# Triangle attention in front of a Mamba-like layer: turned weights in two PSUM banks of their own, projections between a row's other products

## What is computed

```python
q = (xn @ w_q).reshape(B, I, J, H, C) * (1.0 / np.sqrt(C))
k = (xn @ w_k).reshape(B, I, J, H, C)
v = (xn @ w_v).reshape(B, I, J, H, C)
scores = jnp.einsum('bimhc,binhc->bihmn', q, k) + tri_bias + mask_bias
attn = jax.nn.softmax(scores, axis=-1)
o = jnp.einsum('bihmn,binhc->bimhc', attn, v)
g = jax.nn.sigmoid((xn @ w_g + b_g).reshape(B, I, J, H, C))
o = (g * o).reshape(B, I, J, H * C)
return o @ w_o + b_o
...
x = x + _L0_conv_ref(_gn(x), ...)
x = x + _L1_conv_ref(_gn(x), ...)
```

## Time and profile before

| | |
|---|---|
| median of 3 runs | 27614.51 us (27614.04 to 27621.61) |
| profiled execution | 27622.95 us, its span 27621.2 us |
| mean granted TensorE clock | 0.946 |
| busy over the span | PE 79%, DVE 92%, ACT 86%, GpSimd (POOL) 85% |
| attention stage | from about 700 to 2910 us of the span |
| the second layer with the normalisation ahead of it | from 2910 us to the end |

### The profile page before, as it was taken

The page is one execution under the profiler, slowest core; times in us unless marked ns, Lnnn a source line. Parts: engine busy times, 40 slices in busy tenths (PEclk is TensorE's granted clock), DMA queues, the critical chain, the costliest instruction groups (busy, mean ns, idle before and its releaser), DMA issues.

```text
span 27621.2 us, 494663 instructions
## 1 busy us (share of the span) xinstructions
PE 21957.3 (79%) x145198; PEld 16882.3 (61%) x145198; DVE 25285.8 (92%) x23743; ACT 23632.0 (86%) x48522; POOL 23358.9 (85%) x10372
## 2 busy tenths in 40 slices
PE   5888588788887888887888888888788888888887
PEld 1666366666666666666666666666666666666666
DVE  7777599999999999999999999999999999999998
ACT  2677488988989988889898898888898998888988
POOL 4000399999999999999999999999999999999999
PEclk6999799999999999999999999999999999999999
DMA  4111433333333333333333333333333333333333
GB/s 148 48 46 46 150 105 106 107 105 107 106 107 107 107 106 107 106 107 105 107 106 106 106 108 105 108 104 108 105 107 105 108 104 108 106 106 107 106 107 97
DMA packets 2189148, 2868.62 MB, mean 104 GB/s; under 512 B 695002, under 2 KB 964858, under 8 KB 2177786
## 3 DMA queue, kind: packets, MB, share of 16 engines
q1 hardware_dynamic: 2181978, 2803.33, 33.0%
q10 hardware_dynamic: 4608, 33.82, 0.3%
HBM read 2667.01 MB, written 169.74 MB: 103 GB/s over the span
## 4 chain that ended last, share of the span: by engine, by line
ACT 28%; PE 25%; issue 18%; DVE 12%; POOL 4%; ACTq 1%; DVEq 1%; DMA 0%; SPq 0%; POOLq 0%
DVE hst L1530 11%; PE yps L1240 7%; ACT dbT L1420 6%; ACT dA L1398 6%; ACT dAs L1398 6%; PE dbx L1225 5%; PE misc L1140 5%; POOL hc L1607 2%; POOL dbu L1593 2%; DVE hc L1538 2%; ACT vab L1353 1%; PE misc L1159 1%; PE misc L1176 1%; PE cps L1216 1%; ACT vab L1339 1%
## 5 line engine op out<-in xcount | busy, mean ns | idle before, releaser
L1593 POOL TENSOR_TENSOR dbu<-dtu,bb 128x1024 f32<-128x1024 f32 x4096 | 9697.6, 2374 | 1209.2 <-DVE hst L1530 1208.3
L1530 DVE TENSOR_TENSOR_SCAN hst<-dA,dbu 128x1024 f32<-128x1024 f32 x4096 | 9336.8, 2279 | 778.1 <-ACT dA L1398 755.9
L1607 POOL TENSOR_TENSOR hc<-hst,cc 128x1024 f32<-128x1024 f32 x4096 | 9743.1, 2379 | 5.6 <-DVE hst L1530 3.7
L1240 PE MATMUL yps<-ident,hc 128*128 128x128 f32 x65536 | 8944.2, 283 | 328.6 <-POOL hc L1607 325.1
L1240 PEld LDWEIGHTS yps<-ident,hc 128*128 128x128 f32 x65536 | 7982.1, 147 | 1824.7 <-issue 1273.4
L1530 DVE TENSOR_TENSOR_SCAN hst<-dAs,dbx 128x1024 f32<-128x1024 f32 x3584 | 8104.2, 2261 | 63.5 <-issue 61.2
L1225 PE MATMUL dbx<-ident,dbT 128*128 128x128 f32 x28672 | 4153.0, 292 | 3329.9 <-DVE hst L1530 2975.1
L1225 PEld LDWEIGHTS dbx<-ident,dbT 128*128 128x128 f32 x28672 | 3391.2, 148 | 4750.2 <-DVE hst L1530 3639.0
L1420 ACT ACTIVATE dbT<-dtuT,bT 128x256 f32<-128x256 f32 x14336 | 6125.1, 495 | 18.2
L1398 ACT ACTIVATE dA<-dtv,aneg 128x508 f32<-128x508 f32 x8192 | 5291.6, 678 | 400.0 <-DVE hst L1530 396.1
L1398 ACT ACTIVATE dAs<-dtv,aneg 128x508 f32<-128x508 f32 x7168 | 4743.7, 710 | 531.0 <-DVE hst L1530 528.8
(11 more groups left out here) (187 smaller groups left out, 25145.4 us busy)
## 6 DMA issues: line engine op xcount, KB each, us to landing
bb<-l_bscr SPq DMA_DIRECT2D x1024, 1024.0 KB, 5.7
cc<-l_bscr SPq DMA_DIRECT2D x1024, 1024.0 KB, 5.5
bx<-l_bscr SPq DMA_DIRECT2D x1024, 256.0 KB, 6.1
xg<-xgp SPq DMA_DIRECT2D x512, 85.0 KB, 2.5
xgp<-xb ACTq DMA_DIRECT2D x32, 1032.0 KB, 9.4
xt<-in_x_dram SPq DMA_DIRECT2D x128, 256.0 KB, 2.7
l_xnT<-xo SPq DMA_DIRECT2D x128, 256.0 KB, 2.0
xn<-l_xnT SPq DMA_DIRECT2D x256, 128.0 KB, 2.1
```

The source lines that it names most:

```text
L1240: mm = pe.matmul(yps[:, p, f * P:(f + 1) * P], hc[:, u % HB, f * 512 + p * P:f * 512 + (p + 1) * P], ident[:], is_transpose=True, start=fi ...
L1530: nc.vector.tensor_tensor_scan(hst[:, v % 4, way], decays.rearrange("p f c -> p (f c)")[:, way], inputs.rearrange("p f c -> p (f c)")[:, way],
L1593: nc.gpsimd.tensor_tensor(to, dtu[:, step % 2], row.unsqueeze(1).to_broadcast([P, 2, 512]), ALU.mult).then_inc(s_inp, 1)
L1607: nc.gpsimd.tensor_tensor(hc[:, v % HB].rearrange("p (f c) -> p f c", f=2), hst[:, v % 4].rearrange("p (f c) -> p f c", f=2), row.unsqueez ...
```

## The change

It has five parts, all in the attention stage.

1. The turned weights go to banks 6 and 7: heads 0 and 2 to bank 6, heads 1 and 3 to bank 7. Scores keep banks 2 to 5 for themselves and wait for the additions of the row before (`s_sm`), no longer for weight copies. Heads 2 and 3 are turned once heads 0 and 1 are copied. The turned factors share bank 6, the sums share bank 0 with q and k, and the output shares bank 1 with v and gate.
2. VectorE copies heads 0 and 2, ScalarE heads 1 and 3, each between additions or exponentials of the next row.
3. q and k of the next row are projected between heads 1 and 2 of the turned weights, v and gate of the next row at the turn's end; a new stage "next" of a turn does so. SyncE loads `xn` two rows ahead and the mask one row ahead, in two functions.
4. PE's turn begins with the scores. ScalarE's tanh comes first in its turn, the factors' copy ahead of the last exponentials.
5. The residual is added by transposes (`is_transpose=True`) in place of matmuls with the identity.

```diff
-            ps_qk, ps_vg, ps_o, ps_x = (banks[:, b] for b in (0, 1, 6, 7))
+            ps_qk, ps_vg = banks[:, 0], banks[:, 1]
+            ps_out, ps_o = banks[:, 1, 0:N], banks[:, 0, 0:N]
+            ps_f = banks[:, 6, 0:N]
...
+                    def project_qk(r, h):
                         pe.wait_ge(s_xn[h], turns(r, h, 1))
-                        wait(pe, s_qe, r)
+                        wait(pe, s_gs, r - 2)
                         for k in range(2):
                             mm = pe.matmul(ps_qk[:, k * N:(k + 1) * N], wqk[:, k], xn[:, h], start=True, stop=True)
                         mm.then_inc(s_qk, 1)
+                    def project_vg(r, h):
                         wait(pe, s_ve, r * 2)
+                        wait(pe, s_xe, r - 2)
...
                     def scores(r, h):
                         pe.wait_ge(s_mk[h], NH * turns(r, h, 1))
                         pe.wait_ge(s_qe, r + 1)
-                        wait(pe, s_tv, r * 3)
-                        wait(pe, s_ta, r)
+                        wait(pe, s_sm, r * NH)
...
+                    def turned(r, h, d):
+                        pe.wait_ge(s_ex, r * NH + (d + 1))
+                        if d == 0:
+                            wait(pe, s_fc, r)
+                        elif d == 2:
+                            pe.wait_ge(s_tv, r * 2 + 1)
+                        else:
+                            wait(pe, s_ta, r * 2 + d // 2)
+                        for k in range(NT):
+                            for a in range(NT):
+                                mm = pe.transpose(banks[:, 6 + d % 2, (k * NT + a) * P:(k * NT + a + 1) * P],
+                                                  ss[:, h, d, a, k * P:(k + 1) * P], ident0[:])
+                        mm.then_inc(s_tf, 1)
...
-                            pe.matmul(dst, wo0[:], goT[:, h, a * P:(a + 1) * P], start=True, stop=False)
-                            mm = pe.matmul(dst, xr[:, h, a], ident0[:], start=False, stop=True)
+                            pe.matmul(dst, wo0[:], goT[:, h, a * P:(a + 1) * P], start=True, stop=False, skip_group_check=True)
+                            mm = pe.matmul(dst, xr[:, h, a], ident0[:], is_transpose=True, start=False, stop=True, skip_group_check=True)
...
+                        if "new" in stages:
+                            scores(r, h)
+                        if "mid" in stages:
+                            turned(r - 1, 1 - h, 0)
+                            turned(r - 1, 1 - h, 1)
+                        if "next" in stages:
+                            project_qk(r + 1, 1 - h)
+                        if "mid" in stages:
+                            turned(r - 1, 1 - h, 2)
+                            turned(r - 1, 1 - h, 3)
+                        if "end" in stages:
+                            output(r - 2, h)
+                        if "next" in stages:
+                            pe.wait_ge(s_qe, r + 2)
+                        if "mid" in stages:
+                            sums(r - 1, 1 - h)
+                            turn_factors(r - 1)
+                        if "next" in stages:
+                            project_vg(r + 1, 1 - h)
```

More of the change, by code:

```diff
@@ L357, in all_rows @@
             def all_rows(eng, turn):
-                turn(0, 0, ("new",))
-                turn(1, 1, ("new", "mid"))
+                every = ("next", "new", "mid", "end")
+                turn(0, 0, ("next", "new"))
+                turn(1, 1, ("next", "new", "mid"))
                 for r in (2, 3, 4):
[L362 to L365, removed]
+                    turn(r, r % 2, every)
+                with eng.Fori(2, N // 2 - 2) as i:
+                    turn(2 * i + 1, 1, every)
+                    turn(2 * i + 2, 0, every)
+                turn(N - 3, 1, every)
+                turn(N - 2, 0, every)
                 turn(N - 1, 1, ("new", "mid", "end"))
@@ L420, in project @@
                         mm.then_inc(s_vg, 1)
[L422 to L442, removed]
                     def scores(r, h):
@@ L511, in turn, with copy_qk @@
                             wait(act, s_bn, r - 3)
-                            nc.scalar.activation(xo1[:, h], ps_x[:, N:2 * N], ACT.Identity, bias=bo[:]).then_inc(s_xe, 1)
+                            nc.scalar.activation(xo1[:, h], ps_out, ACT.Identity, bias=bo[:]).then_inc(s_xe, 1)
                         if "new" in stages:
[L514 to L526, removed]
+                            weights(2)
+                        if "mid" in stages:
+                            act.wait_ge(s_gt, r)
+                            wait(act, s_gs, r - 1)
+                            nc.scalar.mul(fT[:], ps_f, 0.5).then_inc(s_fc, 1)
+                        if "new" in stages:
+                            weights(3)
+                    def copy_qk(r, h):
+                        act.wait_ge(s_qk, r + 1)
+                        nc.scalar.mul(qk[:, h, 0], ps_qk[:, 0:N], float(-1.0 / HD ** 0.5))
+                        nc.scalar.copy(qk[:, h, 1], ps_qk[:, N:2 * N]).then_inc(s_qe, 1)
+                    copy_qk(0, 0)
                     all_rows(act, turn)
@@ L565, in turn @@
                             nc.vector.tensor_tensor(ge[:, h], vg[:, :, 1], bg[:].unsqueeze(1).to_broadcast([P, NT, P]), ALU.add).then_inc(s_ve, 1)
+                            top(0)
                         if "mid" in stages:
+                            turn_out(0)
                             factors(r - 1, 1 - h)
                         if "new" in stages:
[L569 to L575 removed]
+                            top(1)
+                        if "mid" in stages:
+                            turn_out(2)
+                        if "new" in stages:
+                            top(2)
+                            top(3)
                         if "mid" in stages:
```

91 lines of the change are left out of this document (56 added, 35 removed).

## The result

The changed kernel takes 27468.84 us (median of 5 runs, 27458.93 to 27479.74) against 27616.67 of the kernel before on the same chips: a ratio of 0.9945, interval 0.9931 to 0.9960. That is 148 us less, where the forecast of 27285 took 332 off, and lies above the range that ended at 27400.

A forecast was written before the change was run, and what follows sets the result against it. It took the attention stage's ring of waits over four shared banks, once a turn of 8.60 us, as the bound. Turns of 7.3 gave (8.60 - 7.30) x 256 = 333 us off, so 27285, range 27215 to 27400.

The forecast's parts named there:

- everything behind it is untouched: Code after the attention stage, about 700 to 2910 us, was taken as unchanged, with no time of its own.
- Prologue and tail do the same turns as before: Turns outside the attention loop were taken as unchanged, with no time added.
- The ring: Attention stage: waits from scores through ACT's copies to v and gate, closing last at 7.24 us.
- a restart: PE's sums in the attention turn: 0.10 us added to their 1.00 after the wait.
- which I price the same: PE's scores: 1.30 us kept, with a tile-form change on either side instead of one and a restart.
- 0.2 in two turns for the jump: Where the attention loop comes round: 0.2 us for the jump and its registers, giving 7.34 a turn.
- Dearer handoffs: Rival: waits between engines in the attention stage cost more, 7.75 us a turn, 27397 us; chance 0.16.
- the 6.95 of that rival: Rival: PE bounds the attention turn, 6.83 us of work plus one tile change, 27192 us; chance 0.06.
- The clock rival: Rival: the kernel gets slower through the clock; chance 0.03.
- that of no gain: Rival: fT late on ACT delays gating and bank release, turn back at 8.6 us, 27614; chance 0.03.
- Part (4) at nothing: Residual by transposes on PE: worth 0.22 us a turn, costed at nothing because PE would wait before the sums.
- Part (3) and SP: Heads 2 and 3 wait for copies; SP's mask lands 4.0 us into the turn, needed at 7.2.

The follow-up runs named there:

- e3: The changed kernel with the residual again added by fp32 matmuls in place of transposes; 28137.13 us, ratio 1.0186.
- e5: The changed kernel with 10 extra two-column matmuls (40 PE instructions) behind the attention stage's last product; 28130.21 us, ratio 1.0181.
- e1: The kernel before with two more of its looped turns written out behind the loop; 27991.16 us, ratio 1.0132.
- e8: The changed kernel with new step orders on ACT and DVE and 32 extra matmuls; 27273.01 us, ratio 0.9873.
- e6: The changed kernel with 64 extra two-column matmuls (256 PE instructions) behind the attention stage's last product; 27507.79 us, ratio 0.9956.
- e4: The changed kernel with ACT's exponentials of head 0 moved behind the copy of head 3; 27662.39 us, ratio 1.0015.
- e11: The changed kernel with 20 extra two-column matmuls (80 PE instructions) behind the attention stage's last product; a single run, 27297.12 us.

## Why the prediction was wrong

**The step that failed** is its first: "everything behind it is untouched. So the question is that stage." The source behind it is untouched, but its place isn't. The change adds two written turns and other instructions, and PE's code of the second layer moved from place 243 to 28 of a piece of 256 (my count). The sum had no term for it. The sentence "Prologue and tail do the same turns as before" has the same gap: the turns are the same, and more of them are written out. The move cost 110 us in the profiled executions, of the 184 by which the result missed 27285. That place is the cause, and not what the attention stage does or when it ends, is shown by the pads: 40 idle instructions (4 us) move the second layer from 24529 to 25207, 128 to 24370, and 256 leave it at 24563; the kernel before reacts the same way (24356 and 24545). At one place the change is worth what the stage gives: at 243 and 244, 27357.65 against 27630.97 of the kernel before in the same runs, 273 less; at 27 and 28, 27468.84 against 27759.20, 290 less. Both are more than the 266 of the stage, by 7 and 24 us. Kernels at one place differ by up to 34 us in the second layer, the pads take some of the time themselves (23 us for the 54), and the second pair is from two series of runs, so that no more than "about 270" can be read from it.

How a place turns into time the traces show in part. The profile's queue 8 has pieces of 16384 bytes (21.36 MB / 1304), 1280 in the kernel before, 1304 in the changed one, 1346 in e3. From the page's table of queues (packets, MB, share of 16 engines), the kernel before:

```profile
q8 instruction: 1280, 20.97, 0.3%
```

The changed kernel:

```profile
q8 instruction: 1304, 21.36, 0.3%
```

And e3:

```profile
q8 instruction: 1346, 22.05, 0.3%
```

PE alone has a long jump at the loop's end: 3.6 us, where DVE's takes 0.06 and those of ACT, POOL and SP 0.05, in the source view of the changed kernel's loop line (count, then least, median and most ns):

```profile
L1048 DVEq COMPARE_BRANCH  x126: 50/56/68, 3341.5 to 27241.6; - x126
...
L1048 PEldq COMPARE_BRANCH  x126: 83/3620/5272, 3342.8 to 27243.0; - x126
```

The jump itself lasts about as long before (median 3519 ns) and in e3 (3895, which over 126 passes is some 35 us more than 3620). In all 125 jumps of each trace at least one piece of queue 8 arrives. What differs most is the second pause, which ends some 10 us behind the jump's start, the 3.88 us above. Read in the same way from the packed traces, it is over 2.5 us long in 125 of e3's 125 passes and in 125 of e5's, 575 and 582 us in sum, each time with a piece of queue 8 that ends in it, 1.2 to 1.7 us before PE goes on. In the kernels with 1280 to 1282 pieces there is none. So PE waits at place 68 a second time, behind the jump. That a packet of queue 8 is what it waits for, there and at the jump, is inferred from how the two fall together; no view names a packet as PE's releaser.

For the places between, this is not the whole account. In the traces at 27 and 28 such a pause stands in one pass at most, and at 41 (e1) in four, although the layer is 401 us longer there; the jumps are on average 0.2 to 0.5 us longer than in the kernel before, 30 to 57 us in all. Where the rest of e1's 401 us goes stays open. Nor is it shown what ACT's and DVE's places add; places 243 and 244 are 54 us apart in the profiled executions and some 15 by the medians.

**The ring** was the right one, and its size was short: 7.24 in the straight turn, 7.56 measured, 7.3 taken (7.34 with the jump, rounded down). So 0.26 x 256 = 67 us of the miss are terms that were too small. By the ring's steps, measured against forecast: scores 1.30 as forecast; transposes to ACT's start 11.52 to 12.66 = 1.14 for 1.07; copy 0.48; exponentials 1.00 for 0.99; q and k copies 0.52; copy of head 3 0.60 for 0.58; handoff 15.26 to 15.40 = 0.14 for 0.06; sums 1.00 for 1.10, so that the 0.10 taken for a restart did not show; factors 0.35 for 0.27; v and gate 1.03 for 0.87. The last two are what matters. Half of the 0.16 of v and gate lies between its last pass and the scores (0.31 from start to start, against 0.22 between passes, 0.09 more). I put these 0.09 down to the step "which I price the same", the change from the whole array to row strips ahead of the scores, which before stood within the scores' wait for copies (0.94 in the earlier trace rows); that is my estimate from the two pitches. The other half lies behind the first pass (1.10 busy for four, 1.03 in the earlier trace rows). No run takes these apart. "0.2 in two turns for the jump" was not needed: both turns of the loop take 7.57.

Of the 0.32 by which 7.56 exceeds 7.24 only these 0.09 lie at a change of form. Of PE's four changes in a turn the one ahead of the sums still falls into a wait (0.37).

**The rivals.** Dearer handoffs is the nearest, at 7.56 and not 7.75 a turn. PE was not the bound in the changed kernel (it waits 0.37 a turn ahead of the sums) and is in e8. Its own work was put too low: 6.83 in the prediction, 7.56 - 0.37 = 7.19 in the changed kernel, so that the 6.95 of that rival was out of reach. The clock rival and that of no gain fell: the turn is 7.56, and the granted clock is 1.00 with 20 transposes in it, as it was with 18 before. No run has a lower clock in this stage (1.00 from 800 to 2500 us in each of the thirteen). **Part (4) at nothing** was right while PE waits ahead of the sums (e3, turns 7.55); with the orders of e8, where it doesn't, this was not tried. **Part (3) and SP** were right: no wait for a mask or a bank stands among the stage's long ones.

## What to carry to other kernels

Read the time of the unchanged code too, before and after: here it moved by up to 851 us with the place of a loop in PE's stream, while the change itself was worth 270. Before a reordering is judged by its whole time, try it with two or three pads (128 instructions are half of the 256 after which the time came back in e6), or compare the stages and the count of queue 8's packets on the two pages. And lay a change in a ring of three engines out as a timetable over more than one turn: it gave 8.2 for e4, where the shortened ring alone would have promised 7.2, and it found the order of e8.

## What the runs showed of the hardware

- The same second layer takes 24356 to 25207 us (190 to 197 us for each of the 126 passes of its loop), by where PE's code of it starts, counted in 256 instructions: 24356 to 24419 at 108 to 244, rising over 28 (24529) and 41 (24821) to 68 (25196 and 25207), and at 24357 again at 108 (e11).
- The slower places show 1301 to 1346 packets of 16384 bytes in queue 8, the faster ones 1280 to 1282.
- At the worst place (e3, e5) 125 passes have a second stop of PE, 4.6 us on average, that ends about 10 us behind the start of the jump; a packet of queue 8 ends 1.2 to 1.7 us before PE goes on.
- The jump at the end of that loop takes PE 3.6 us (median, the changed kernel), DVE 0.06.
- From v and gate (whole array) to the scores (row strips) it is 1.03 us in the changed kernel, where four passes of that size needed 0.87 ahead of other whole-array work in the earlier trace rows.
- With 20 transposes in a turn of 7.56 us (16 of weights, two of factors, two of the residual) the granted clock was 1.00 from 800 to 2600 us.
